# A third message pass with its softmax weights also in PSUM, and the eight PSUM banks dealt out anew

## What is computed

```python
xh = (x @ W).reshape(N, H, D)
a_src = jnp.einsum('nhd,hd->nh', xh, att_src)
a_dst = jnp.einsum('nhd,hd->nh', xh, att_dst)
e = jax.nn.leaky_relu(a_src[src] + a_dst[dst], NEG_SLOPE)
m = jax.ops.segment_max(e, dst, num_segments=N)
e = jnp.exp(e - m[dst])
denom = jax.ops.segment_sum(e, dst, num_segments=N)
alpha = e / denom[dst]
msg = xh[src] * alpha[:, :, None]
out = jax.ops.segment_sum(msg, dst, num_segments=N).reshape(N, H * D) + bias
```

## Time and profile before

| | us |
|---|---|
| median of three runs | 5766.87 |
| profiled execution | 5758.8 |
| its span, first to last instruction | 5757.0 |
| busy: POOL | 3830.7 |
| busy: PE matmul | 3694.3 |
| busy: DVE | 3292.2 |
| busy: ACT | 1396.5 |
| third pass, gathers of POOL from first to last | 3481.7 to 4549.3 |

### The profile page before, as it was taken

How to read it: one execution, slowest core, us unless ns; L and a number is a source line. 1 busy time by engine, 2 the same in 40 slices (tenths; PEclk the granted TensorE clock), 3 DMA queues, 4 the chain that set the end, 5 groups by cost and what they waited for, 6 DMA issues and landing times. The chain is left out here.

```text
span 5757.0 us, 117872 instructions
## 1 busy us (share of the span) xinstructions
PE 3694.3 (64%) x13068; PEld 2405.3 (42%) x13069; DVE 3292.2 (57%) x11050; ACT 1396.5 (24%) x4357; POOL 3830.7 (67%) x4008
## 2 busy tenths in 40 slices
PE   4514676667664697366666665777777626666667
PEld 1402333333344343244444444666666514443445
DVE  7415666666653232355555556777777775555556
ACT  0302333333343110000000034666666320000002
POOL 2765766666667777777777716777777437777773
PEclk8755777777777898677777787988888766777778
DMA  1202444444410343344454423444444235444443
GB/s 54 73 20 63 104 95 98 94 95 91 91 37 3 109 153 119 65 111 111 112 112 112 112 81 85 110 109 109 109 109 109 70 88 112 111 111 111 111 111 98
DMA packets 1094228, 543.72 MB, mean 94 GB/s; under 512 B 905512, under 2 KB 991231, under 8 KB 1093882
## 3 DMA queue, kind: packets, MB, share of 16 engines
q0 software_dynamic: 177920, 424.21, 26.6%
q1 hardware_dynamic: 556152, 105.79, 9.2%
q10 hardware_dynamic: 360064, 12.78, 3.5%
HBM read 458.47 MB, written 83.62 MB: 94 GB/s over the span
## 5 line engine op out<-in xcount | busy, mean ns | idle before, releaser
L1245 PE MATMUL psS_plain_src<-got_plain_src,hot_plain_src 128*128 x3328 | 1318.7, 547 | 820.2 <-SPq L1084 591.1
L1245 PEld LDWEIGHTS psS_plain_src<-got_plain_src,hot_plain_src 128*128 128x128 f32 x3328 | 813.5, 266 | 1325.8 <-issue 1201.0
L1142 DVE TENSOR_TENSOR sums<-sums,psS_plain_src 128x257 f32 x1664 | 700.5, 421 | 874.8 <-PE psS_plain_src L1245 708.2
L1104 POOL DMA_INDIRECT got_edge_mlp_dst<-dram_ptab,tile_rec_edge_mlp_dst x784 | 743.1, 948 | 424.0 <-DMA tile_rec_edge_mlp_dst<-dram_rec_dst 213.6
L518 POOL DMA_INDIRECT dram_rec_src<-rec_src x784 | 766.9, 978 | 340.0 <-issue 253.2
L644 POOL DMA_INDIRECT got_attend_dst<-dram_gtab,recs_attend_dst x832 | 814.9, 979 | 254.5 <-issue 175.2
L1104 POOL DMA_INDIRECT got_plain_src<-dram_htab,tile_rec_plain_src x784 | 744.4, 949 | 241.7 <-issue 215.7
L1104 POOL DMA_INDIRECT got_plain_src<-dram_xtab,tile_rec_plain_src x784 | 743.4, 948 | 241.8 <-issue 219.4
L1264 PE MATMUL psS_edge_mlp_dst<-msg_edge_mlp_dst,hot_edge_mlp_dst 128*128 128x256 f32 x1664 | 690.0, 555 | 179.7 <-DVE sage_sums L1142 118.6
L839 PE MATMUL psS_attend_dst<-msg_attend_dst,hot_attend_dst 128*128 128x264 f32 x1664 | 611.2, 454 | 39.3 <-DVE msg_attend_dst L725 21.2
L1264 PEld LDWEIGHTS psS_edge_mlp_dst<-msg_edge_mlp_dst,hot_edge_mlp_dst 128*128 128x128 f32 x1664 | 388.2, 262 | 405.1 <-issue 177.6
(11 more groups left out here) (331 smaller groups left out, 3873.3 us busy)
## 6 DMA issues: line engine op xcount, KB each, us to landing
dram_xtab<-out_tab SPq DMA_DIRECT2D x48, 1024.0 KB
recs_plain_src<-dram_rec_src ACTq DMA_DIRECT2D x1664, 4.0 KB
tile_rec_plain_src<-dram_rec_src SPq DMA_DIRECT2D x1568, 4.0 KB
recs_edge_mlp_dst<-dram_rec_dst ACTq DMA_DIRECT2D x832, 4.0 KB
recs_attend_dst<-dram_rec_dst SPq DMA_DIRECT2D x832, 4.0 KB
got_attend_dst<-dram_gtab,recs_attend_dst POOLq DMA_INDIRECT x832
dram_rec_src<-rec_src POOLq DMA_INDIRECT x784
tile_rec_edge_mlp_dst<-dram_rec_dst SPq DMA_DIRECT2D x784, 4.0 KB
```

The lines of the kernel that those rows point to most:

```text
L1104: nc.gpsimd.indirect_dma_start(got[:, u, 0:width], None, table, bass.IndirectOffsetOnAxis(tile_rec[:, u, index_word:index_word + 1].bitcas ...
L1142: nc.vector.tensor_tensor(here, here, psS[t[1] % banks][:, 0:cols], ALU.add).then_inc(added, 1)
L1245: nc.tensor.matmul(psS[t[1] % banks][:, 0:cols], hot[:, t[1], :], flat[:, bass.ds(slots.of(u), cols)], start=True, stop=True).then_inc(sum ...
```

## The change

The exp L806 is issued twice per pair: first into columns 32 to 47 of the pair's `psN` bank, then, as before, into `msg`. The message L725 takes its weights from that bank in place of `msg`. Since the weights live there until the message is made, `psN` has four banks in place of two, and the node terms wait for the messages four pairs back. To make room, `psS` has three banks in place of four, with 16 not a multiple of 3, so that tile 0 of a round waits for the add of the tile right before it; and `psF` has one bank in place of two, so that each transpose waits for the copy of the tile right before it.

```diff
-            psF = [pt("psF0"), pt("psF1")]
-            psN = [pt("psN0"), pt("psN1")]
+            psF = pt("psF")
+            psN = [pt(f"psN{k}") for k in range(4)]
...
-            banks = 4
+            banks = 3
             psS = [pt(f"psS{k}") for k in range(banks)]
+
+        def bank_back(t):
+
+            return {0: 1, 1: 4, 2: 4}.get(t[1], 3)
+
+        def weights(t):
+
+            return psN[t[1] // 2 % 4][:, 4 * HEADS:6 * HEADS].rearrange("p (t w) -> p t w", t=2)
...
-                        n = psN[k][:, 0:4 * HEADS].rearrange("p (t w) -> p t w", t=2)
+                        n = psN[scores[1] // 2 % 4][:, 0:4 * HEADS].rearrange("p (t w) -> p t w", t=2)
...
                             got[:, t[1], 0:D].rearrange("p (h d) -> p h d", d=DH),
-                            msg[:, t[1] % 8, D:AW].unsqueeze(2).to_broadcast([P, HEADS, DH]), ALU.mult).then_inc(msgs, 1)
+                            weights(t)[:, t[1] % 2, :].unsqueeze(2).to_broadcast([P, HEADS, DH]), ALU.mult).then_inc(msgs, 1)
...
                         m = t[1] % 8
+                        nc.scalar.activation(weights(t), z[:, t[1] // 2 % 2, :, :], ACT.Exp)
                         nc.scalar.activation(msg[:, m - 1:m + 1, D:AW], z[:, t[1] // 2 % 2, :, :], ACT.Exp).then_inc(ws, 1)
...
-                        nc.scalar.copy(hotT[:, t[1] % 4, :], psF[t[1] % 2][:, 0:P]).then_inc(hotTs, 1)
+                        nc.scalar.copy(hotT[:, t[1] % 4, :], psF[:, 0:P]).then_inc(hotTs, 1)
...
-                wait_count(pe, added, ring.count(t, banks))
+                wait_count(pe, added, ring.count(t, bank_back(t)))
...
-                        done = pairs_done(t, 2)
-                        wait_count(pe, zchain, None if done is None else 3 * done)
-
-                        nc.tensor.matmul(psN[t[1] // 2 % 2][:, 2 * HEADS * (t[1] % 2):2 * HEADS * (t[1] % 2 + 1)],
+                        done = pairs_done(t, 4)
+                        wait_count(pe, msgs, None if done is None else 2 * done)
+                        nc.tensor.matmul(psN[t[1] // 2 % 4][:, 2 * HEADS * (t[1] % 2):2 * HEADS * (t[1] % 2 + 1)],
...
-                        wait_count(pe, hotTs, ring.count(t, 2))
-                        nc.tensor.transpose(psF[u % 2][:, 0:P], hot[:, u, :], c.ident[:, :]).then_inc(turned, 1)
+                        wait_count(pe, hotTs, ring.count(t, 1))
+                        nc.tensor.transpose(psF[:, 0:P], hot[:, u, :], c.ident[:, :]).then_inc(turned, 1)
```

## The result

The changed kernel takes 5924.9 us (median of five runs, 5918.4 to 5929.1), the kernel before 5766.9 beside it: 1.0275 times as long (95% interval 1.0261 to 1.0289), +158 us. The forecast was 5887, in a range of 5790 to 5965. The profiled execution took 5923.5 us with a span of 5921.8, 164.8 more than before, and nearly all of the difference lies in the third pass: from the first gather to the end of the last add it takes 1076.6 us before and 1235.2 after, +158.6.

The account below looks back on a forecast made before the run. POOL was taken as the bound, 20.54 us per round; the loop would take over at 21.1 + 0.28 x 6.2 = 22.8, 2.3 more times 52 = +120 us: 5758.8 becomes 5879, plus 8.1 gives 5887. Range 5790 to 5965.

Parts of the forecast that it names:

- The other engines' loop: Third pass, ACT, PE and DVE waiting for each other: 4.47 us per four tiles, against 5.00 for undisturbed POOL.
- The two rivals below 5790 us: Third pass: loop stays under POOL's 5.0 us per group, 5748, chance 0.08; or no difference, 5767, chance 0.07.
- Rival 1: Third pass: same loop with the clock always full, +30 us, 5797; chance 0.14.
- Rival 2: Third pass: same loop, half of the groups at half rate, 24.2 us per round, +190, 5957; chance 0.21.
- The operand: POOL's gathers, no longer lengthened by the message L725 with weights in PSUM: 18.8 us less for POOL.
- Plain group: Third group of a round, the loop without extra terms: 4.75 us at full clock, 6.37 at half.
- Second exp: ACT, one added exp per group ahead of the copy, on the loop: +0.11 us.
- four banks: Node terms wait for messages four pairs back, done by the start of `rel`: costs nothing.
- Three banks: Tile 0's sums wait for the previous tile's add: next scores about 0.16 us late, fourth group 5.33 us.
- First group: First four tiles of a round, with PE's register load in the loop: 5.8 us at full clock, 7.3 at half.
- the register load: PE, once per round behind tile 15's transpose: next sums start 1.08 us behind it, now inside the loop.
- What would show it: Signs in the changed profile: POOL idle on messages, copy waits in nearly all 208 groups, `psN` wait up 100 us or more.

Follow-up runs that it names:

- l1: Changed kernel with the third pass's gather cut to 8 scores per row: 5918.4 us, 1.0276 times the full kernel before.
- l2: Kernel before with one transpose bank alone, third pass's gather cut to 8 scores per row: 5863.3 us, 1.0175 times the full kernel before.
- e6b: Changed kernel with PE's load of 16 registers split, 3 at step 0, 13 at step 3: 7754.2 against 7597.9 us for the kernel before, 1.0207.

## Why the prediction was right, and where it was off

**Direction and mechanism: right, and shown.** The forecast was +120 us and the measured change is +158. The other engines' loop was the near second bound; the edit to make room (one transpose bank) lengthened it past POOL's 20.0 us per round; POOL then waited for messages. The two rivals below 5790 us (the loop stays under POOL; no difference) fall with POOL's 239.8 us of waits. Rival 1 (clock always full, 5797) falls with the granted clock of 0.82. Rival 2 (clock lower than now, half of the groups at half rate, 5957) came true in part: the granted clock fell from 0.86 to 0.82, and the transpose of tile 4g ran at half clock in 71 of 198 groups, 36%, where before it was 56, or 28%. The measured 5925 lies 38 us above the forecast and 32 below this rival.

**The operand: right, and without value.** Forecast 18.8 us less for POOL: 814.9 to 796.2 is 18.7. Behind the first eight gathers, the excess over 0.947 us per gather fell from 20.9 to 2.2 us, near the 2.4 that was to stay. It is worth nothing where POOL waits. The message itself, forecast within 10 ns of 418, takes 412.

**Plain group: right.** Forecast 4.75 at full clock, measured 4.61 (median of 49 third groups); the transpose is released 0.06 us behind the copy's end and not 0.13. One reading behind it was wrong: in the kernel before the transpose of tile 4g-1 was not done long before R; by medians it started at R-0.47, R+1.20, R+0.18 and R+0.27 in the first to fourth group. It stood off the loop all the same, since the transpose of tile 4g waited for the one-hots until R+2.48 to R+2.97 (medians).

**Second exp, four banks: right.** 0.12 against 0.11 us per group; PE has no idle time ahead of the node terms.

**Three banks: undersized.** I had 0.16 in the fourth group; l1 against l2 has 0.46, of which 0.12 is the exp, so about 0.34. In the sum over 52 rounds that is 9 us more. It is a difference of two kernels that differ in the four banks for node terms as well.

**First group: the step that was mis-sized.** I took the register load at 1.08 us from the earlier trace rows and had 5.8 us at full clock, 7.3 at half. Measured 7.70 on average. The load was counted from the wrong event. The earlier trace rows has the distance from the transpose of tile 15 to the next weight load; the transpose had been released earlier, by the end of the copy of tile 13:

```profile
3809.93 0.27 ACT L810 COPY hotT_attend_dst<-psF_attend_dst 128x128 f32<-128x128 f32 x1 [0.51 <-PE psF_attend_dst L862]
```

That copy ends at 3810.20, and the next sums' weight load starts at 3812.13, 1.93 us later. In the changed kernel the copy of tile 14 ends at 4078.66 and the weight load starts at 4080.59, again 1.93 us later. The distance from the end of the releasing copy is 1.93 to 1.95 us in 47 of 50 rounds before and in 48 of 50 after. So the load with what stands around it takes the same time in both kernels. In the kernel before the released transpose started 0.85 us behind the copy, PE being still busy with matmuls queued ahead of it, and only 1.08 stuck out; in the changed kernel it starts 0.05 us behind the copy, and 1.88 stick out. In the sum that is 0.8 us per round, 42 us, more than the 38 by which the forecast was short.

The half clock isn't spread over the groups as I had it. It comes behind this stall: in the first group the transpose of tile 0 ran at half clock in 47 of 50 rounds (before in 26), and it stands at R+5.18, which is 1.97 + 1.88 + 1.33, where I had 0.6 for the last step. In the third groups it ran so in 3 of 49. I had taken 0.28 of all groups; the released transposes of tile 4g-1 ran at half clock in 22 of 50 second groups, 1 of 49 third ones and 4 of 49 fourth ones. So an underestimate of the first group (7.70 against a mix of 6.2), by the load and by the clock, and an overestimate of the third and fourth (4.69 and 5.55 against 5.2 and 5.9) partly cancelled: 23.5 us per round against 22.8. That the forecast came within 38 us is in part luck.

**What would show it, as listed.** Gathers over 0.975 us fell from 156 to 21; POOL's idle time rose by 169 us, and its releaser is the message; the third group is 4.61; the mean clock is 0.82. Two items were off: DVE's wait for `psN` rose by 54 us, not 100 or more (its waits for sums rose by 80 beside it), and L870 waits for the copy 157 times, not in nearly all 208 groups.

## What to carry to other kernels

When two bounds lie within 10% of each other, an edit that relieves the first must be costed on the second, by the chain that closes on itself there, every wait of it. Taking a double buffer away ties two engines step by step, and each step then stands in the order of the slower queue; look for what else stands behind the new wait in that queue (here a register load once per round). A stall measured behind queued work is only the part that sticks out: to price it, measure from the event that released the instruction ahead of it, here the end of the copy (1.93 us before and after), and not from that instruction's start (1.08 and 1.88).

## What the runs showed of the hardware

- With a load of 16 registers from SBUF between them, PE's next weight load starts 1.93 us after the end of the copy that releases the transpose ahead, in the kernel before as after (47 and 48 of 50 rounds). For 3 registers it is 1.55 us (e6b). The part that shows behind the transpose is 1.08 us before and 1.88 after. A load of 13 at another step showed 2.92 us, unexplained.
- A gather issued on POOL takes 951 to 957 ns on average with the message's second operand in PSUM and 978 to 986 with both in SBUF, on the chip with the kernel before at 5761 us and in the main runs, whatever its rows' size (32 or 1056 bytes: 952 and 957, 986 and 979 ns). With both in SBUF and the message running 0.1 us into the gather, it took 1.03 us on average and up to 1.21 (230 gathers).
- The same kernel took 5761 us on one chip and 7598 to 7739 on three others, with POOL's instruction at the same 947 ns and the same code. What differed in the traces was the rate of the transfers, 83 against 111 GB/s in the fourth pass, and POOL's waits for records. On two of those the single transpose bank cost 0.75 and 0.72%, where it cost 1.75% on the fast one (l2, with the light gather, which by itself changed nothing there: 1.0003). A loss in the order of the engines can partly hide below slower transfers.
